# Keeping the scan's output in SBUF instead of parking it in HBM, and one block per half

## The reference

```python
xn = _layernorm(x)                                  # x: [8, 2048, 1024], f32
# recurrence: y_t = tanh(a) * y_{t-1} + b * xn_t, per channel, then a projection
scan = einsum('btd,ed->bte', y, w_out) + b_out
# transformer, 2 layers, 8 heads of 64, window 512, hidden 2730
for l in range(2):
    h = shift_token(z); q, k, v = split(h @ wqkv[l])
    q, k = l2norm(q) * qs, l2norm(k) * ks; q, k = rotary_xpos(q, k)
    z = z + local_attention(q, k, v) @ wo[l]        # z starts as xn
    h = layernorm(shift_token(z)) * lg + lb
    a, g = split(h @ w1[l] + b1[l])
    z = z + (a * gelu(g)) @ w2[l] + b2[l]
out = x + scan + z
```

## Time and profile before

| | us |
|---|---|
| median of 3 runs | 3165.91 |
| lowest and highest of them | 3154.68, 3209.14 |
| profiled execution | 3152.98 |
| its span on the slowest core (core 1) | 3151.4 |
| spans of the eight cores | 3139.8 to 3151.4 |
| mean granted TensorE clock of the eight cores | 0.737 to 0.742 of 2.4 GHz |

### The profile page before, as it was taken

The page is one execution under the profiler, slowest core; times in us unless marked ns, Lnnn a source line. Parts: engine busy times, 40 slices in busy tenths (PEclk is TensorE's granted clock), DMA queues, the critical chain, the costliest instruction groups (busy, mean ns, idle before and its releaser), DMA issues. The chain is left out here.

```text
span 3151.4 us, 27882 instructions; the slowest of 8 cores (3139.8 to 3151.4 us)
## 1 busy us (share of the span) xinstructions
PE 2080.5 (66%) x9488; PEld 936.2 (30%) x9488; DVE 1094.3 (35%) x1849; ACT 602.1 (19%) x1016; POOL 38.9 (1%) x58
## 2 busy tenths in 40 slices
PE   1055667599866675998113566767997577759992
PEld 1022233144322331443111123332442223324441
DVE  4612444511215446111365044444111244462112
ACT  1021332211022321110021133212100133312100
POOL 0001000000010000000000000000000000000000
PEclk9988555699985556999557865557998855579995
DMA  4135960021359700212522410010222300002225
GB/s 91 56 87 68 112 75 8 27 80 56 59 60 110 85 1 27 80 54 75 158 74 74 54 20 1 1 27 27 74 60 41 40 1 1 1 27 67 60 61 160
DMA packets 128463, 176.51 MB, mean 56 GB/s; under 512 B 48723, under 2 KB 91220, under 8 KB 127108
## 3 DMA queue, kind: packets, MB, share of 16 engines
q0 software_dynamic: 31776, 56.62, 15.0%
q1 hardware_dynamic: 96548, 118.11, 13.0%
HBM read 210.34 MB, written 52.42 MB: 83 GB/s over the span
## 5 line engine op out<-in xcount | busy, mean ns | idle before, releaser
L332 ACT ACT_TABLE_LOAD x67 | 86.0, 1283 | 1275.3 <-PE psA L1201 368.6
L1620 PE MATMUL psB<-stg,WS 128*128 128x512 bf16 x704 | 278.0, 395 | 48.1 <-ACT stg L332 48.1
L1624 PE MATMUL psB<-stg,WS 128*128 128x512 bf16 x704 | 278.6, 396 | 0.0
L1620 PE MATMUL psA<-stg,WS 128*128 128x512 bf16 (+1 forms) x704 | 269.6, 383 | 0.0
L1624 PE MATMUL psA<-stg,WS 128*128 128x512 bf16 (+1 forms) x704 | 269.2, 382 | 0.0
L1641 PE MATMUL psA<-Bb,WS 128*128 128x512 bf16 x1024 | 232.7, 387 | 11.1 <-DVE UN L332 11.1
L1201 PE MATMUL psA<-Bb 64*128 64x128 bf16 (+3 forms) x432 | 179.3, 415 | 34.6 <-ACT probs L332 29.6
L332 DVE TENSOR_TENSOR UN<-UN 128x1024 bf16<-128x1024 bf16 (+1 forms) x56 | 51.5, 920 | 398.5 <-ACT UN L332 322.2
L332 ACT ACTIVATE probs<-psA 128x640 bf16<-128x640 f32 (+5 forms) x264 | 171.3, 649 | 95.3 <-PE psA L1201 66.9
L1240 PE MATMUL psB<-attnT,Bb 128*64 128x128 bf16 x960 | 79.1, 311 | 144.0 <-DVE attnT L332 144.0
L891 PE MATMUL psA<-stg,WS 128*128 128x512 bf16 x512 | 135.7, 427 | 37.8 <-DMA WS<-wqkv 21.7
(11 more groups left out here) (118 smaller groups left out, 2456.7 us busy)
## 6 DMA issues: line engine op xcount, KB each, us to landing
WS<-wpre SPq DMA_DIRECT2D x184, 256.0 KB, 3.0
wpre<-w1p POOLq DMA_DIRECT2D x8, 2730.0 KB, 71.1
WS<-wpre SPq DMA_DIRECT2D x96, 224.0 KB
UN<-x SPq DMA_DIRECT2D x32, 512.0 KB, 4.6
WS<-wqkv POOLq DMA_DIRECT2D x24, 512.0 KB, 7.3
wpre<-w2p POOLq DMA_DIRECT2D x4, 2730.0 KB, 145.7
park<-UN SPq DMA_DIRECT2D x16, 512.0 KB, 2.9
Bb<-park SPq DMA_DIRECT2D x16, 512.0 KB
```

What stands on the lines that cost most here:

```text
L332: ins = f(*a, **kw)
L1620: t.matmul(rA[0:ln, tc * 512:(tc + 1) * 512], wu[:, kt * ln:(kt + 1) * ln], B.stg[kt][:, tc * 512:(tc + 1) * 512], start=(kt == 0), stop=( ...
L1624: ins = t.matmul(rG[0:ln, tc * 512:(tc + 1) * 512], wu[:, 1024 + kt * ln:1024 + (kt + 1) * ln], B.stg[kt][:, tc * 512:(tc + 1) * 512], sta ...
```

## The change

The scan's output stays on the chip. Eight tiles `parkSB[g]` (128 x 1024, bf16) are added; ScalarE evicts chunk `ec` into `parkSB[ec]`, the park writes and the waits on them are gone, and with them the read-back in `phase_final`, where VectorE now adds `parkSB[g]` and `u[g]`. The scan's output is thus rounded to bf16 once. The two blocks of a half become one. In place of the meeting at the end of the first block, three waits order layer 1 behind layer 0: SyncE's column loads wait for the last residual and the last GELU of the FFN, and GpSimd's first two QKV weight loads for the last two W2 chunks. The wait for the park writes before the QKV apply is dropped.

```diff
--- before.py
+++ after.py
@@ -162,6 +162,7 @@
         def sb(name, shape, dty):
             return st.enter_context(nc.sbuf_tensor(name, shape, dty))
         self.u = [sb(f"u{g}", [128, H + 1], F32) for g in range(NG)]
+        self.parkSB = [sb(f"parkSB{g}", [128, H], BF16) for g in range(NG)]
         self.stg = [sb(f"stg{g}", [128, H], BF16) for g in range(NG)]
         self.Bb = [sb(f"Bb{i}", [128, H], F32) for i in range(NG)]
         self.tabsb = sb("tabsb", [128, 4 * H], BF16)
@@ -411,18 +412,13 @@
             with B.nc.Block() as b1:
                 phase_p0(B, h, b1)
                 phase_scan(B, h, b1)
-                phase_qkv(B, h, 0, b1)
-                phase_attn(B, h, 0, b1)
-                phase_wo(B, h, 0, b1)
-                phase_ln(B, h, 0, b1)
-                phase_ffn(B, h, 0, b1)
-            with B.nc.Block() as b2:
-                phase_qkv(B, h, 1, b2)
-                phase_attn(B, h, 1, b2)
-                phase_wo(B, h, 1, b2)
-                phase_ln(B, h, 1, b2)
-                phase_ffn(B, h, 1, b2)
-                phase_final(B, h, b2)
+                for l in range(NL):
+                    phase_qkv(B, h, l, b1)
+                    phase_attn(B, h, l, b1)
+                    phase_wo(B, h, l, b1)
+                    phase_ln(B, h, l, b1)
+                    phase_ffn(B, h, l, b1)
+                phase_final(B, h, b1)
 
     with B.nc.Block() as blk:
         @blk.sync
@@ -689,7 +685,6 @@
         ev_dma = [None] * 8
         ev_mm = [None] * 8
         ev_evac = [None] * 8
-        pk_base = B.sP.n
 
         def issue_wout(s, ec):
             if ec >= 2:
@@ -729,26 +724,18 @@
 
                 sc = B.S
                 B.w(sc, "scalar", ev_mm[ec])
-                if ec >= 1:
-                    B.w(sc, "scalar", (B.sP, pk_base + 16 * ec))
                 reg = B.psb(0 if ec % 2 == 0 else 2, 1024)
                 ev_evac[ec] = B.ev(B.sS, sc.activation(
-                    B.un(PKS, 1024), reg, AF.Identity,
+                    B.parkSB[ec][:], reg, AF.Identity,
                     bias=B.boutc[:, ec:ec + 1]))
 
             B.scan_evac = ev_evac
             B.scan_mm = ev_mm
 
-            @blk.sync
-            def _(s):
-                if ec + 2 < 8:
+            if ec + 2 < 8:
+                @blk.sync
+                def _(s):
                     issue_wout(s, ec + 2)
-                B.w(s, "sync", ev_evac[ec])
-                B.ev(B.sP, s.dma_start(
-                    out=B.d_park[ec * 128:(ec + 1) * 128, t0:t0 + H],
-                    in_=B.un(PKS, 1024)), 16)
-                if ec == 7:
-                    B.park_done = B.mark(B.sP)
 
 
 def _load_cols_layer(B, s, l):
@@ -833,6 +820,8 @@
 
         @blk.sync
         def _(s):
+            if l == 1:
+                B.w(s, "sync", *B.ffn_done_evs)
             B.lcols_ev = _load_cols_layer(B, s, l)
 
         @blk.vector
@@ -856,6 +845,8 @@
         def issue_qkv_group(g, grp):
             if l == 0 and grp < 2:
                 B.w(g, "gpsimd", B.scan_mm[6 + grp])
+            if l == 1 and grp < 2:
+                B.w(g, "gpsimd", B.w2mm_pred[7 - grp])
             c0 = grp * 2
             gi, par = B.ws.issue(g, [(
                 B.wsb(B.ws.idx % 2)[:, 0:2048],
@@ -987,7 +978,7 @@
                 def _(v, qk=qk, g_=g_, c=c):
                     v = B.V
                     B.wf(v, "vector", B.qs8_ev)
-                    B.w(v, "vector", bc_ev[c], qraw_ev[c], B.park_done)
+                    B.w(v, "vector", bc_ev[c], qraw_ev[c])
                     bc = B.psB[:, 1024:2048]
                     scal = B.qs8 if qk == 0 else B.ks8
                     apply_ev[c] = B.ev(B.sV, v.scalar_tensor_tensor(
@@ -1578,9 +1569,11 @@
         mm_pred = [(B.sT, tbase + j + 1) for j in range(NHCH)]
         w2mm_pred = [(B.sT, tbase + NHCH + m + 1) for m in range(8)]
         B.w2mm_pred = w2mm_pred
+        B.ffn_done_evs = None
         gel_pred = [(B.sS, sbase + j + 1) for j in range(NHCH)]
         gate_pred = [(B.sV, vbase + j + 1) for j in range(NHCH)]
         w2res_pred = [(B.sV, vbase + NHCH + m + 1) for m in range(8)]
+        B.ffn_done_evs = (w2res_pred[7], (B.sS, sbase + NHCH))
 
         @blk.sync
         def _(s):
@@ -1686,32 +1679,20 @@
     XTI = [4096, 5120]
 
     with _maybe_block(nc, blk_) as blk:
-        pk_ev = [None] * NG
         sum_ev = [None] * NG
         tp_ev = [None] * 8
         add_ev = [None] * 8
         x_ev = [None] * 8
         st_ev = [None] * 8
 
-        @blk.sync
-        def _(s):
-            B.w(s, "sync", B.park_done)
-            B.wf(s, "sync", B.w2mm_pred[7])
-            for g in range(NG):
-                B.ev(B.sX, s.dma_start(
-                    out=B.Bb[g][:, 0:H],
-                    in_=B.d_park[g * 128:(g + 1) * 128, t0:t0 + H]), 16)
-            for g in range(NG):
-                pk_ev[g] = B.mark(B.sX)
-
         for g in range(NG):
             @blk.vector
             def _(v, g=g):
 
                 v = B.V
-                B.w(v, "vector", pk_ev[g])
+                B.wf(v, "vector", B.w2mm_pred[7])
                 sum_ev[g] = B.ev(B.sV, v.tensor_add(
-                    B.Bb[g][:, 0:H], B.Bb[g][:, 0:H], B.u[g][:, 1:H + 1]))
+                    B.Bb[g][:, 0:H], B.parkSB[g][:], B.u[g][:, 1:H + 1]))
 
         def issue_xf(s, tb):
             if tb >= 2:
```

## The result

The changed kernel takes 3069.76 us in the median of 10 runs, the kernel before 3153.46 in the median of 10 beside it; the ratio of the two is 0.973 with a 95% interval of 0.972 to 0.975. The profiled execution took 3070.34 us, its slowest core spans 3068.7.

The account below looks back on a forecast made before the run. It took a chain of stages, each bounded by its last-ending wait; 37.9 + 46.6 + 2.0 = 86.5 us off the profiled 3152.98 gave 3066.5, off the shown runs 3079 and 3068; forecast 3070 us, range 3048 to 3096.

Parts of the forecast that it names:

- part 1: Final stage without the read-back: the sums follow the last residual directly, 19.5 and 18.4 us gained, together 37.9 us.
- part 4: Layer boundary, one block instead of two: 1.0 us gained per boundary, 2.0 us in all, ends 0.3 and 4.5.
- Part 2: Scan without park writes: evictions no longer wait, a chunk takes 3.6 us; its gain is counted in Part 3's 46.6 us.
- Part 3: SyncE's queue after the scan: column loads start earlier, so ScalarE starts QKV 23.8 and 22.8 us sooner, together 46.6 us.
- rival A: Scan to QKV: column loads meet weight loads and take 26 us; sum 72.1, time 3081; chance with its twin 0.20.
- Part 5: The dropped park wait before the QKV apply gains nothing, since the last park write had long landed.
- B: QKV starts: column and weight loads get out of each other's way, first chunk gates everywhere; 95.9 us, time 3057; chance 0.14.
- C: QKV and attention: TensorE loses its high clock; at 1.2 GHz throughout 208 us are lost, time 3275; chance 0.03.
- D: Final stage: the read-back was hidden anyway, so part 1 brings nothing, time 3104; chance 0.02.
- The first sum: Sign in the final stage: it follows the last residual by 0.1 us and takes about 1.2 us.
- the pace of the chunks: Sign in the scan: 16-matmul chunks start 3.45 to 3.7 us apart, with no eviction waiting on a DMA.
- the wait on b1g: Sign at the scan's step into QKV: ScalarE still waits on b1g, 18 to 20 us from the first column load.

Follow-up runs that it names:

- b1: The kernel before with layer 0's column loads issued ahead of the scan's matmuls, park writes and read-back kept; ratio 0.992 to the kernel before.
- b2: The kernel before with only the two blocks of a half made one, with the change's three waits; ratio 0.998 to the kernel before.
- e2: The changed kernel with a read of 8 x 512 KB from HBM put back before the final sums; 3094 us, ratio 0.981 to the kernel before.
- e3: The changed kernel with layer 0's column loads held back until the scan's last eviction; ratio 0.977 to the kernel before.
- e4: The changed kernel with layer 0's column loads issued ahead of the scan's matmuls; 3056 us, ratio 0.969 to the kernel before.
- the repeat: The changed kernel itself, run and profiled again on the chip of a later run; ratio 0.972 to the kernel before.
- e6: e5 plus scales and biases of both layers loaded once ahead of the first scan; 2983 to 2988 us, ratio 0.946 to the kernel before.
- e5: The changed kernel with eight buffers for x in the final stage instead of two; 3014 to 3016 us, ratio 0.956 to the kernel before.

## Why the prediction was right, step by step

The time is 3069.76 against 3070 predicted, the ratio's interval is clear of 2%. The sum of 86.5 us stands against 82.7 between the spans of the two slowest cores and 85.6 in the mean over the cores. The mechanisms are those of the prediction; that the total is so near is partly luck. Two terms missed in opposite ways, part 1 by -3.9 and part 4 by +3.4 us. And 3070 is not the sum, which gave 3066.5: I had gone 3.5 us above it because the first three runs had a median of 3165.91, above the profiled execution. In ten runs that median is 3153.46, and the 3.5 us happened to cover what the sum had too much.

*Part 1, final stage, 37.9 predicted, 34.0 in the mean.* The mechanism is that of the prediction: the wait is gone, the sums take its place at once, the two x loads are off the path and eight mixed sums take 10.53 us, just what the f32 ones took the earlier trace rows. The size was off by 4 us, since I took the waits of the slowest core for those of all. The wait also changes from execution to execution: over the cores b1 and b2 have 31.8 and 30.1 us for the same two reads, e2 29.4 for its own. So 34.0 is the high end of what these traces show for the read-back.

*Part 2, the scan's chunks.* 3.45 us each in the first half (ScalarE's table loads at 171.44 and 174.89) where I took 3.6; in the second one chunk on core 3 waited 0.63 us for its weights. So the rate was TensorE's with the weight load just behind it, as argued. Only the first chunk was slower, 6.3 us to ScalarE's table load against 5.4 before (161.71 to 167.99 and 161.79 to 167.17), which took back what 3.45 for 3.6 had given.

*Part 3, 46.6 predicted, 45.6 in the mean.* Column loads at 185.62 (predicted 185.4), GpSimd's weights at 189.18 (188.9). The open number was how long it is from the first column load to ScalarE's start: 18.8 taken, 21.4 us in the first half and 16.5 in the second on core 3, 19.6 and 17.8 over the cores, 18.7 in the mean. The weights took 11.7 us to the first matmul in the first half on core 3 against 8.5 taken, 9.3 and 7.9 over the cores. So what looked like rival A on the slowest core is the spread between cores. b1 and e3 show the queue's place as a cause by itself, which the sum had as one with the loop.
The Trainium skill's page DMA: Bandwidth & Descriptors, section Issuing engines are not separate DMA queues, has both kinds of transfer on the same engines. By that rule the runs agree: with the column loads out of the way the same weight load was there in 7.0 us instead of 11.7 on core 3 (e4), and in 6.6 and 6.0 instead of 9.3 and 7.9 over the cores.

*Part 4, the merge, 2.0 predicted, 5.4 in the first trace, 2.9 in the repeat, 3.9 in b2.* I had priced the block end and left the head start of the weight loads at a guess. It is 1 to 2 us a boundary; whether the head start is all of it stays open.

*Part 5, nothing,* holds: outside the three steps the eight cores differ by 0.6 us in the mean.

*The rivals.* A (column loads of 26 us) did not come on any core. B (everything gets out of the way) did not come: ScalarE still ends its wait on b1g in all four QKV stages, if only about 1 us behind the first chunk in the scan step; e6 is the kernel in which it comes. C did not come: the granted clock is 0.743 to 0.747 over the cores, against 0.737 to 0.742, and in the first 72 us of the four QKV stages 0.88 to 0.91 against 0.87 to 0.90, on the slowest cores. D is refuted by e2: a read of that size in that place costs 24 to 30 us.

*The signs.* The first sum, the pace of the chunks and the wait on b1g came as named. Three lengths on core 3 did not: from the first out-projection matmul to ScalarE's table load it is 45.3 and 41.1 us, not 42 to 43 (43.1 and 41.1 over the cores), from the first column load on 21.4 and 16.5, not 18 to 20, and from a boundary's last residual 16.1 and 15.8, not 17 to 19. Such waits on a single core were not to be told to 1 us; in the mean the sum had them right.

## What to carry to other kernels

Read a wait together with the queue in which its transfer stood: the eleven small loads were needed only at QKV, but stood behind eight stores that waited for evictions, and that was worth 24 us by itself. A store that is later read back costs three times: the wait of whoever reuses its buffer, the queue it stands in, and the read. And size a DMA wait from all cores, and from more than one execution: on the slowest core such waits happened to be long here, 38.2 us of read-back against 34.2 over the cores. When a wait ends later than everything else, look also at what its engine does right after it: here 1.64 us of small work stood behind it and was gone once the wait was.

## What the runs showed of the hardware that I had not expected

Eleven loads of 34 KB in all take 12.3 us by themselves, and beside two loads of 512 KB up to 21.4 us in the changed kernel's trace, 19.6 and 17.8 over its cores. They stretch the larger load as well: from its issue to the first matmul it is 9.3 and 7.9 us with them and 6.6 and 6.0 without (e4). The single issue of `b1a` then holds SyncE for 7.18 us (in the time line after).

Sixteen matmuls took 3.61 us after 3.27 us of idling (e4, core 3) and 5.37 after 8.84 (changed). But the wait ahead does not settle it alone. In the changed kernel all sixteen first chunks, after 3.6 to 8.8 us, took 5.1 to 6.2 us; in e4, after 2.5 to 4.2 us, five of sixteen took 3.61 and the others 4.9 to 6.5. In the mean that is 4.9 instead of 5.6 us.

In e5 the eight output stores go out at the pace of VectorE's adds (six in 8.10 us, the adds 1.22 us each with 0.17 to 0.59 between them), and all eight stores of 512 KB have landed 15 us after the first was issued (1473.75 to 1488.86, where SyncE's next load had waited for them). The loop of the changed kernel moved one load and one store in about 6 us.
